# Low halves of the gate and up weights in batch 0's routed bodies: made by VectorE in place of GpSimd

## What is computed

```python
x = x + tanh(g_xattn[0]) * xattn(ctx_1024, layernorm(x), ...)   # in_proj, conv, x_proj, selective scan over L, * silu(z)
x = x + tanh(g_ffn[0]) * ffn(layernorm(x), ...)

def _fused_linear(x, W, qa, qb, scale, w):
    out = x @ W.T
    a = jnp.einsum('th,krh->tkr', x, qa)
    b = jnp.einsum('tkr,khr->tkh', a, qb)
    return out + scale[None, :] * jnp.einsum('tkh,tk->th', b, w)

# ffn: top-6 of 64 places, 8 experts, and a shared expert
gate = silu(_fused_linear(xe, gW, gqa, gqb, gs, w)); up = _fused_linear(xe, uW, uqa, uqb, us, w)
out  = _fused_linear(gate * up, dW, dqa, dqb, ds, w)
```

## Time and profile before

| | us |
|---|---|
| median of 3 runs | 1644.08 (1643.93 to 1644.24) |
| profiled execution | 1648.37 |
| its span | 1646.5 |
| PE busy in the span | 1539.3 (93%) |
| DVE busy | 1160.1 (70%) |
| POOL busy | 732.9 (45%) |
| ACT busy | 656.3 (40%) |

### The profile page before, as it was taken

One profiled execution on the slowest core, in us unless ns is written; L12 is line 12 of the kernel. 1 busy time (PEld: TensorE's weight loads), 2 busy tenths in 40 slices (PEclk: granted clock), 3 DMA queues, 4 the chain that ended last, 5 costly groups with the idle time before them and its releaser, 6 DMA issues.

```text
span 1646.5 us, 19454 instructions
## 1 busy us (share of the span) xinstructions
PE 1539.3 (93%) x6728; PEld 1134.1 (69%) x6728; DVE 1160.1 (70%) x1635; ACT 656.3 (40%) x1035; POOL 732.9 (45%) x536
## 2 busy tenths in 40 slices
PE   5678699898888899999999999999999999999999
PEld 3334477666666677777777778777777777777776
DVE  6899864898999857588988755788898553333333
ACT  7555344544454433444444344434443321111111
POOL 3589310688888801167778301377787000000000
PEclk9799899999999999999999999999999999999999
DMA  7799437688888674765667445577765556466652
GB/s 260 263 331 312 179 131 250 215 287 295 273 283 290 232 271 166 256 218 203 211 235 250 173 166 189 205 270 244 257 206 178 185 191 211 165 213 209 215 188 80
DMA packets 118930, 368.60 MB, mean 224 GB/s; under 512 B 21072, under 2 KB 48720, under 8 KB 103600
## 3 DMA queue, kind: packets, MB, share of 16 engines
q1 hardware_dynamic: 109360, 333.54, 58.4%
q10 hardware_dynamic: 9472, 33.82, 6.3%
HBM read 297.78 MB, written 68.16 MB: 222 GB/s over the span
## 4 chain that ended last, share of the span: by engine, by line
PE 62%; DVE 17%; issue 6%; ACT 5%; DMA 4%; POOL 4%; SPq 1%; DVEq 0%; ACTq 0%; POOLq 0%
PE b_g L773 15%; PE b_u L773 14%; PE b_u L865 8%; DVE ring L1547 5%; PE b_q L819 4%; PE b_g L865 4%; PE b_q L865 3%; DVE ring L1553 3%; PE b_g L837 3%; PE b_g L804 2%; POOL ring L1446 2%; DMA raw<-in_gu 2%; DVE tt L1521 2%; DMA qat<-scr_qa 2%; PE b_g L797 1%
## 5 line engine op out<-in xcount | busy, mean ns | idle before, releaser
L1446 POOL TENSOR_TENSOR ring<-du,rep 128x512 f32<-128x512 f32 x256 | 345.0, 1356 | 112.8 <-DVE du L1626 81.9
L773 PE MATMUL b_g<-xnb,gm 128*128 128x512 f32 (+1 forms) x1440 | 359.4, 398 | 1.0 <-DVE xnb L1524 0.9
L773 PE MATMUL b_u<-xnb,gm 128*128 128x512 f32 (+1 forms) x1440 | 349.9, 392 | 0.6 <-DVE xx L1521 0.6
L1455 POOL TENSOR_TENSOR yx<-yx,ring 128x512 f32<-128x512 f32 x192 | 261.8, 1363 | 128.8 <-DVE ring L1553 128.0
L773 PEld LDWEIGHTS b_g<-xnb,gm 128*128 128x128 f32 (+1 forms) x1440 | 253.1, 180 | 92.0 <-issue 27.2
L1547 DVE TENSOR_TENSOR_SCAN ring<-b_a,ring 128x512 f32<-128x512 f32 x256 | 310.7, 1214 | 5.5 <-ACT b_a L1012 3.7
L773 PEld LDWEIGHTS b_u<-xnb,gm 128*128 128x128 f32 (+1 forms) x1440 | 256.8, 179 | 73.4 <-DVE xx L1521 2.0
L1012 ACT ACTIVATE b_a<-delta,a_neg 128x512 f32<-128x512 f32 x256 | 173.2, 680 | 96.2 <-DVE ring L1547 96.2
L1521 DVE SCALAR_TENSOR_TENSOR tt<-tt,b_g 128x512 f32<-128x512 f32 (+1 forms) x120 | 82.0, 684 | 181.8 <-ACT tt L1012 181.6
L865 PE MATMUL b_u<-dwt,hhl 128*128 128x512 f32 (+1 forms) x720 | 191.1, 395 | 0.8 <-issue 0.7
L1012 ACT ACTIVATE tt<-b_g 128x512 f32<-128x512 f32 (+1 forms) x120 | 71.1, 593 | 266.2 <-PE b_u L804 235.3
(11 more groups left out here) (249 smaller groups left out, 2076.5 us busy)
## 6 DMA issues: line engine op xcount, KB each, us to landing
gm<-scr_gm SPq DMA_DIRECT2D x64, 1024.0 KB, 9.1
dwt<-scr_dw SPq DMA_DIRECT2D x32, 1536.0 KB, 6.6
rep<-bc_d ACTq DMA_DIRECT2D x64, 512.0 KB, 6.8
gm<-scr_gm SPq DMA_DIRECT2D x32, 768.0 KB, 4.6
scr_gm<-gm SPq DMA_DIRECT2D x20, 1024.0 KB, 7.9
dqt<-scr_dq SPq DMA_DIRECT2D x25, 640.0 KB, 8.4
qat<-scr_qa SPq DMA_DIRECT2D x25, 512.0 KB, 9.8
raw<-in_gu SPq DMA_DIRECT2D x16, 704.0 KB, 8.2
```

The costliest lines, as they stand in the source:

```text
L773: i = mm(out_b[0:IW[m], :], w, v, start=(n == 0), stop=(n == 11 and not is_routed(s)))
L1446: v.tensor_tensor(ring_at(nb, T), du[:, T % 4, :], rep[:, N % NREP, 0], ALU.mult).then_inc(pool_dbu, 1)
L1455: v.tensor_tensor(yd, yd, ring[:, T % NRING], ALU.add).then_inc(pool_y, 1)
```

## The change

Three of the seven low halves of a body move from POOL's order to DVE's: gm0 after the low half of the hidden chunk 1, ahead of slot "c"; gm1 behind slot "c"; gm2 behind `daw_low`, ahead of qb. It is so in the bodies with s + 1 from 3 to 9, that is e = 0 to 6 of batch 0: 21 instructions. DVE's `lo_piece` is the one that it already uses for the other four. One wait is added on ACT, in the set-up: the rounding of the state rows of batch 0 waits for act_gw to reach 3, which DVE's low half of the router's weights (gwx) raises.

```diff
             def state_rows(nb):
                 act.wait_ge(pe_xd, nb + 1)
+                if nb == 0:
+                    act.wait_ge(act_gw, 3)
                 rounded(s_r, ba[0][:]).then_inc(act_sr, 1)
...
@@ GpSimd
                     if e == 0:
                         if split_here:
                             scale("dq", s)
-                        if split_next:
-                            lo_piece("gm0", s + 1)
                         dbu(nb, 0)
                         dbu(nb, 1)
                     for j in range(n):
                         if split_here and e > 0 and j == 2:
                             scale("dq", s)
-                        if split_next and e > 0 and j == at[0] + 1:
-                            lo_piece("gm0", s + 1)
-                        if split_next and j == at[2]:
-                            lo_piece("gm1", s + 1)
                         if split_next and j == at[3]:
                             scale("qb", s + 1)
                         tile_step(nb, first_tile(e) + j)
-                    if split_next:
-                        lo_piece("gm2", s + 1)
...
@@ VectorE, routed(b, e)
                 hidden(s, 1, mid("h1"))
+                if split_next:
+                    lo_piece("gm0", s + 1)
                 slot("c")
+                if split_next:
+                    lo_piece("gm1", s + 1)
...
                 slot("e")
                 daw_low(s)
+                if split_next:
+                    lo_piece("gm2", s + 1)
...
                 if split_next:
                     lo_piece("qb", s + 1)
                 slot("f")
```

More of the change, by code:

```diff
@@ L1391, in lo @@
                 return v.tensor_tensor(out_, whole, hi_.bitcast(F32), ALU.subtract)
[L1393 to L1397, removed]
             def parts_0(n):
```

## The result

| | before | after |
|---|---|---|
| median of 4 runs, us | 1644.01 (1643.23 to 1644.24) | 1670.55 (1668.69 to 1672.74) |
| ratio | | 1.0163, interval 1.0145 to 1.018 |
| profiled span, us | 1646.5 | 1667.8 |
| batch 0's bodies 1 to 6, us | 251 | 277 |
| DVE busy there, us | 227.3 | 257.8 |

What follows compares the result with a forecast made beforehand. The prediction took DVE's queue to bound batch 0's bodies 1 to 6. Own work 18.9, memory turns +5, idle filled -4.7 and body 0 at 0 gave +19.2 us, 1663 us; range 1644 to 1676, the forecast's own 1653 to 1673.

Steps and rivals of the forecast that it cites:

- The chain: Batch 0's bodies 1 to 6: DVE's queue sets the time, POOL runs beside it and PE waits for DVE.
- Own work: DVE's queue in the six bodies: the moved low halves add their undisturbed durations, 18.9 us.
- Idle filled: DVE's gaps before chunk 2's tt and before qbt close, taking up 4.7 us.
- Body 0: First routed body of batch 0: added low halves and relieved softplus additions sum to 0 us.
- The edits at no cost: Set-up and SP: ACT's added wait and the changed order of weight loads delay nothing.
- Turns at the memory: Six bodies: change in DVE's waits for POOL's instructions at the shared memory, taken as +5 us.
- The upper end: Memory waits: each operation behind another two-input one pays 1.06 us, gm1 nothing, dqt is relieved; +14.5 us.
- The lower end: Memory waits: they shrink in proportion to POOL's busy time, a factor of 0.81; in sum -3 us.
- By itself it is worth nothing: POOL's queue in the six bodies: the 40.9 us of operations taken away were not on the chain.
- The port as the bound: Rival: the shared memory port limits the six bodies, so the change is faster, 1630.5 us; chance 0.14.
- No change: Rival: the added work hides in DVE's idle time or PE is the limit, 1644 to 1647 us; chance 0.09.
- Dearer: Rival: gm1 and qbt also pay 1.06 us in each body, 12.7 us more, 1674 to 1680 us; chance 0.08.

Runs made afterwards that it cites:

- narrow_after: Changed kernel with POOL's two tile operations of batch 1's scan cut to 32 of 512 columns: 1633.79 us, the kernel before 1644.90.
- hold2_after: Changed kernel with POOL waiting, before four additions and three inputs a body, for DVE's low halves: 1642.30 us, the kernel before 1645.35.
- gm0_only: Kernel before with only gm0's low half moved to DVE, plus ACT's added wait: 1658.32 us, the kernel before 1644.74.
- gm1_only: Kernel before with only gm1's low half moved to DVE, plus ACT's added wait: 1647.73 us, the kernel before 1644.74.
- gm2_only: Kernel before with only gm2's low half moved to DVE, plus ACT's added wait: 1657.27 us, the kernel before 1644.74.
- hold_before: Kernel before with POOL waiting, before its additions at tiles 4 and 9, for DVE's low halves of qa and qb: 1645.70 us, without them 1646.21.

## Why the prediction was right in direction and 7 us short

**The chain.** Right: DVE's queue was the limit of the six bodies. DVE is busy 257.83 - 227.27 = 30.6 us longer and 277 - 257.8 = 19.2 us idle where it was 23.7; 30.6 - 4.5 = 26.1, the bodies' 26.

**Own work, 18.9 us.** Right in size, as narrow_after (1233 and 959 ns) and hold2_after (1218 for 128x1024) show. What it leaves of DVE's 30.6 us is 11.7 us of waits; added up instruction by instruction the waits grow by 12.7.

**Idle filled, -4.7 us.** Right: -4.5, and the gaps are those that were named; tt's of chunk 2 and qbt's idle time in the earlier trace rows is 0.0 after.

**Body 0, 0 us.** Right, +0.5, and the parts are near those counted: body 0 changes by -2.2 us in gm0_only, +0.1 in gm1_only and +2.9 in gm2_only, where -2, +1 and +1 were put down. **The edits at no cost.** In the six bodies DVE's low halves of gm idle 0.3 us in all, so neither ACT nor SP's loads fell behind. In the set-up the rounding of the state rows (in order of time, as the earlier trace rows) starts long after gwx and waits for PE:

```profile
29.84 0.42 DVE L1512 TENSOR_TENSOR gwx<-cs,gwx 128x256 fp32r<-128x256 f32 x1
...
33.76 0.60 ACT L1012 ACTIVATE ring<-b_a 128x512 fp32r<-128x512 f32 x1 [0.44 <-PE b_a L657]
```

**Turns at the memory, +5 us: the term that was put too low.** It measured +11.7, inside its ends of -3 and +14.5 and near the upper one. By groups, against their own price or against before: gm0 and gm1 21.7 - 12 x 1.22 = +7.1 (6.0 of it at gm0, 1.1 at gm1 in one body), gm2 11.0 - 6 x 0.955 = +5.3, dwt +6.0, qbt 8.5 - 6.3 = +2.2, dqt 6.5 - 11.1 = -4.6, the rest together -3.2; that is 12.8, and 11.7 in the stretch, where neighbours overlap. The upper end was a list of payers, gm0, gm2, dwt at 1.06 us each and dqt relieved, gm1 free, and it was right name by name: 6.0, 5.3 and 6.0 where 6.4 was put down for each. The lower end was wrong in kind. It let the waits go down with POOL's busy time, and POOL did work less, by 25 us, and waited six times as long for DVE's ring products, while DVE's waits rose by half. A POOL that has caught up is released by each ring product, and the next of its tiles meets just the burst that stands behind the product; a POOL that lags comes later, or stands before its gm and lets dwt pass. "Near the middle: the bodies have both patterns" was the choice that cost 7 us. Before, one body of the six had the pattern from which the upper end was read: body 3 of the earlier trace rows, where dqt takes 1.08 us; in the other five it meets POOL's gm0 and takes 1.59 to 2.33. After, all six have it: dqt takes 1.08 us, and gm0 and dwt pay, in each. What the change does to POOL's lag decides between the ends, and the prediction named that (dwt "will meet POOL's tiles") without letting it choose. POOL itself paid in the same coin, which is most of why its busy time fell by 25 and not by 40.9 us: its inputs and additions became longer by 13.5 us, the inputs (ring) from 1407 to 1582 ns (the earlier trace rows and here):

```profile
L1442 POOL TENSOR_TENSOR ring<-du,rep 128x512 f32<-128x512 f32 x56 | 88.6, 1582 | 5.3
L1451 POOL TENSOR_TENSOR yx<-yx,ring 128x512 f32<-128x512 f32 x60 | 88.2, 1471 | 78.2 <-DVE ring L1541 78.2
```

**"By itself it is worth nothing."** Wrong: with gm on POOL cut to 8 columns the kernel gains 10.7 us. This gain is inside the result; the work and the turns together cost more than it.

**The rivals.** The port as the bound, 1630.5 us, did not come, though its two halves exist apart: the freed POOL is worth 10.7 us, and POOL held out of the bursts takes DVE's waits from 39.5 to 6.2 us, below the 11.5 from which it was to decide. It needed POOL to come behind DVE's instruction each time; it does so at best for the first of a burst. The Trainium skill (GPSIMD Engine Reference, Key points) has VectorE about twice as fast at elementwise work. The durations agree, 2459 ns on POOL and 1218 on DVE undisturbed; the time does not follow, since DVE was the chain and POOL was not. No change, 1644 us, fell with DVE's idle time, of which only 4.5 us were to be had. Dearer, 1674 us or more, was half there: qbt pays, but 2.2 us more than before and not 6.4, and gm1 pays in one body of six.

## What to carry to other kernels

Where two engines take turns at the memory, price an instruction by what stands in front of it on its own queue: first behind the instruction that releases the other engine it is free if the other had caught up and stood waiting; second or later it waits for the end of one of the other's instructions, here about 1 us, whatever its own size. Less work on the other engine does not mean fewer collisions when that engine is released in step with yours; look for a stall of it that kept it away, and ask what the change does to that stall. If the other engine has time to spare, a wait on it for the end of the burst can pay: here it gave back 29.6 us where the move had lost 26.5. It must stand in front of the very operation that meets the burst; one tile too late it did nothing for qat (hold_before).

## What was not expected of the hardware

A two-input operation of 8 columns lasted 1.26 us behind hhl and 0.15 us behind a ring product, 792 ns in the mean of eighteen. Work on POOL can also cost DVE time without lying on its chain: the long low halves there were worth 10.7 us to a DVE that never waited for their results. And the granted clock of TensorE in the six bodies was 0.91 of full speed in the mean in the changed kernel (0.97 before), full speed (2.4 GHz) with stretches at half of it (1.2 GHz), with PE waiting longer for DVE and its busy time up from 221.6 to 228.6 us; since PE was not the limit in these bodies, DVE's waits for its results stayed at some tenths of a us.
